# Another order for the instruction lists of the front phase of a four-part transformer kernel

## The chip, the cores and the metric

The kernel runs on one NeuronCore of a Trainium2 chip. A core has five engines with an instruction list each: TensorE (PE), VectorE (DVE), ScalarE (ACT), GpSimd (POOL) and the sync engine (SP), which here only starts transfers. An engine takes its own list strictly in order; engines meet at semaphores. The metric is device time in microseconds (us) of one launch. Three runs of the kernel before took 638.17, 638.5 and 638.55 us.

## The reference

Input is `x` of 16 sequences by 64 tokens by 256 features (1024 rows) and a context of the same size. Four blocks follow one another, each with a layer norm in front and a gate `tanh(g)` on what it adds to `x`:

```
x = x + tanh(g_xattn[0]) * attention_0(layernorm(x), mask, ctx)      # one head, 64 keys, new K and V fill the cache
x = x + tanh(g_ffn[0])   * ffn_0(layernorm(x))                       # ternary weights, tokens rounded to 8 bits
x = x + tanh(g_xattn[1]) * attention_1(layernorm(x), ctx)            # 16 query heads of 128, self and cross, fp8 rounding
x = x + tanh(g_ffn[1])   * experts(layernorm(x))                     # 7 routed experts, top 3, and a shared one
```

`ffn_0` is `h = silu(q(x) @ Wg) * (q(x) @ Wu)`, an RMS norm with a weight, and `q(h) @ Wd`. `q` rounds a row to integers by its largest magnitude; the weights are rounded to -1, 0 and 1 by their mean magnitude. In `attention_1` every head of q and k is layer-normed, and `ctx @ w_kv_x` gives the keys and values of the cross attention.

## The kernel before

The program has three phases with a barrier between them: `front` (lines 605 to 1414), two passes of `grouped_attention`, and the experts. The front computes the first attention and the ternary FFN, and beside them three things that the passes need: the rounded inputs `xq` of the first pass, the split weights of that pass (`weights.*`), and the context product (`context(e)`), whose 24 tiles go to memory over SP. The diff touches the front's five lists and nothing else.

The 1024 rows are handled as two groups `s` of four tiles `j`. Helper functions are one step each, and a list is a sequence of calls:

- PE: `turn` (transposes of the normed tokens, L1204), `project_qk` (L1214), `scores` (L1234), `project_v` (L1222), `turn_probs` (L1244), `attend` (L1251), `turn_integers` (L1265), `gate_up(s, n)` (n = 0 to 7, one half row-tile each, L1280), `turn_hidden` (L1294), `down` (L1306), `context(e)` (L1323), `turn_normed` (L1332).
- ACT: `keep_*` empties PSUM banks, `tern.column_sum` and `tern.scale` prepare the ternary weights, `weights.high` makes the upper part of a weight (L195), `gated` is the silu (L1057), `square` (L1064), `over_scale` (L1095).
- DVE: `ln.moments` and `ln.apply` are the layer norm, `weights.mean` (L178, L180) and `weights.low` (L202) prepare a weight, `context_mean` (L900, L902), `hidden(s, n)` multiplies silu and up (L863), `hidden_largest` (L868), `round_hidden` (L889), `add_attention` (L833), `add_ffn` (L895), `round_two` (L908 to L921).
- POOL: `ln.on_pool` (L555), `weights.centre` (L185), `weigh(s, j)` (h times the RMS weight, L750), `centre_context` (L755), `rms` (L759).
- SP: `dma_start` for all inputs, then the 24 stores of `kept`.

The waits that matter for the order: `hidden(n)` waits for `gated(n)`; `gated(n)` waits for `gate_up(n)` and for `hidden(n-2)`; `gate_up(n)` waits for `hidden(n-2)`, since two pairs of PSUM banks alternate. `context(e)` waits for `keep_context(e-2)`. `weigh(s, j)` waits for `square(s, j)`, and `hidden_largest(s, j)` for `weigh(s, j)`. `down(s, j)` needs `keep_hidden(s, j)`, which needs `turn_hidden` and that `round_hidden(s, j)`. `gate_up(0, 0)` needs `tern.clip` 0 and 1. `over_scale` needs `inv`, the reciprocal of the input scales.

Of the kernel before, what the change touches and what calls it, by code (L numbers as in the profile page):

```python
# [21 lines left out]
P = 128  # L22
# [582 lines left out]
def front(nc, t, k, weights, slots):  # L605
# [5 lines left out]
    with phase_semaphores(nc) as take, ExitStack() as c:  # L611
# [93 lines left out]
        def _(sp):  # L705
            source = t["x"].rearrange("(n p) e -> p n e", p=P)
            sp.dma_start(k['x'][:, 0:ST, :], source[:, 0:ST, :]).then_inc(x_loaded[0], 16)
            sp.dma_start(k['x'][:, ST:TILES, :], source[:, ST:TILES, :]).then_inc(x_loaded[1], 16)
# [8 lines left out]
            weights.load(sp, t, 0)  # L717
            sp.dma_start(mask[:], t['mask'].rearrange('(n p) s -> p n s', p=P)).then_inc(q['v_loaded'], 16)
            for n, src in enumerate(('L1_q_in_scale', 'L1_k_in_scale', 'L1_v_in_scale', 'L1_qx_in_scale')):
                sp.dma_start(ins[:, n * KT:(n + 1) * KT], t[src]).then_inc(q['ln_loaded'], 16)  # L720
            sp.dma_start(w_ctx[:, 2], t['L1_wkvxT'][:, 2 * CH:3 * CH].rearrange('(c p) f -> p c f', p=P)).then_inc(q[f'wctx_loaded{2}'], 16)
            sp.dma_start(wv[:], t['L0_WvT'].rearrange('(c p) f -> p c f', p=P)).then_inc(q['v_loaded'], 16)
            weights.load(sp, t, 1)
            sp.dma_start(w_ctx[:, 0], t['L1_wkvxT'][:, 0 * CH:1 * CH].rearrange('(c p) f -> p c f', p=P)).then_inc(q[f'wctx_loaded{0}'], 16)
            sp.dma_start(lnw[:], t['L0_lnw'].rearrange('(o n) -> o n', o=1).broadcast_to([P, INNER])).then_inc(q['lnw_loaded'], 16)
            sp.dma_start(bv[:], t['L0_bv'].rearrange('(o n) -> o n', o=1).broadcast_to([P, E])).then_inc(q['v_loaded'], 16)
            tern.on_sync(sp, t)
            weights.load_small(sp, t)
            weights.load(sp, t, 2)
            sp.dma_start(ctxT[:], t['ctxT'].rearrange('(c p) n -> p c n', p=P)).then_inc(q['ctx_loaded'], 16)  # L730
            weights.load(sp, t, 3)
            sp.dma_start(w_ctx[:, 3], t['L1_wkvxT'][:, 3 * CH:4 * CH].rearrange('(c p) f -> p c f', p=P)).then_inc(q[f'wctx_loaded{3}'], 16)
            sp.dma_start(w_ctx[:, 1], t['L1_wkvxT'][:, 1 * CH:2 * CH].rearrange('(c p) f -> p c f', p=P)).then_inc(q[f'wctx_loaded{1}'], 16)
            for n in range(4, len(weights.kinds)):
                weights.load(sp, t, n)
            for e, (tile, chunk) in enumerate(PRODUCTS):
                sp.wait_ge(q['ctx_kept'], e + 1)
                sp.dma_start(k['kvx'][tile, :, chunk * CH:(chunk + 1) * CH], kept[:, e % 4, :]).then_inc(stored[e % 4], 16)
# [6 lines left out]
        def _(pool):  # L745
# [24 lines left out]
            weights.centre(pool, 0)  # L770
            ln.on_pool(pool, 1)
            weights.centre(pool, 1)
            ln.on_pool(pool, 2)
            ln.on_pool(pool, 3)
            weights.centre(pool, 2)
# [3 lines left out]
            weights.centre(pool, 3)  # L779
            weights.centre(pool, 4)  # L780
            weigh(0, 2)
            weigh(0, 3)
            weigh(1, 0)
            centre_context(0)
            rms(0)
            weights.centre(pool, 5)
# [9 lines left out]
        def _(dve):  # L796
# [131 lines left out]
            weights.mean(dve, 0)  # L928
            ln.apply(dve, 1, lambda j: an[:, 1, j, :])
            weights.mean(dve, 1)  # L930
# [3 lines left out]
            divide(0)  # L934
            add_attention(0)
            ln.moments(dve, 2)
            dve.wait_ge(q['gate_made'], 1)
            weights.scale(dve)
# [4 lines left out]
            weights.low(dve, 0)  # L943
            product_scales(0)
            less_max(1)
            keep_values(1)
            round_tokens(0)
            tern.clip(dve, 0)
            divide(1)
            tern.clip(dve, 1)  # L950
            add_attention(1)
# [5 lines left out]
            weights.mean(dve, 2)  # L957
            hidden(0, 2)
            token_scales(1)
            hidden(0, 3)  # L960
            weights.low(dve, 1)
            round_tokens(1)
            weights.mean(dve, 3)
            hidden(0, 4)
            hidden(0, 5)
            weights.mean(dve, 4)
            hidden_largest(0, 0)
            hidden(0, 6)
# [12 lines left out]
            hidden_largest(0, 3)
            hidden(1, 2)
            mean_square(0)
            hidden(1, 3)
            hidden_largest(1, 0)
            hidden_scales(0)
            hidden(1, 4)
            hidden(1, 5)
            weights.low(dve, 2)
            round_hidden(0, 0)  # L990
            weights.low(dve, 3)
            hidden(1, 6)
            round_hidden(0, 1)
            hidden(1, 7)
            round_hidden(0, 2)
            round_hidden(0, 3)
            weights.low(dve, 4)
            mean_square(1)
            hidden_largest(1, 1)
            hidden_largest(1, 2)  # L1000
# [5 lines left out]
            round_hidden(1, 1)  # L1006
            ln.apply(dve, 4, lambda j: qn[:, 0, j, :])
            round_hidden(1, 2)
            round_hidden(1, 3)
            weights.low(dve, 5)  # L1010
            round_two(0)
# [7 lines left out]
        def _(act):  # L1019
# [81 lines left out]
            keep_qk(0, 1)  # L1101
            keep_tokens(1)
# [4 lines left out]
            tern.column_sum(act, 0)  # L1107
            tern.column_sum(act, 1)
            keep_qk(1, 0)
            tern.column_sum(act, 2)  # L1110
            keep_qk(1, 1)
            weights.high(act, 0)
# [11 lines left out]
            keep_context(3)  # L1124
            gated(0, 2)
            weights.high(act, 1)
            keep_context(4)
            gated(0, 3)
            keep_context(5)
            weights.high(act, 2)  # L1130
            gated(0, 4)
            gated(0, 5)
            square(0, 0)
            square(0, 1)
            keep_context(6)
            keep_context(7)
            gated(0, 6)
            square(0, 2)
            keep_context(8)
            gated(0, 7)  # L1140
            keep_integers(1)
            keep_context(9)
            weights.high(act, 3)
            gated(1, 0)
            square(0, 3)
            gated(1, 1)
            keep_context(10)
            square(1, 0)
            gated(1, 2)
            keep_context(11)  # L1150
            weights.high(act, 4)
            keep_context(12)
            gated(1, 3)
            keep_context(13)
            square(1, 1)
            gated(1, 4)
            gated(1, 5)
            weights.high(act, 5)
            keep_context(14)
            square(1, 2)  # L1160
            gated(1, 6)
            keep_context(15)
            keep_hidden(0, 0)
            gated(1, 7)
            square(1, 3)
            keep_hidden(0, 1)
            keep_hidden(0, 2)
            keep_context(EARLY)
            keep_context(17)
            keep_hidden(0, 3)  # L1170
            keep_context(18)
# [5 lines left out]
            over_scale(1)  # L1177
            keep_hidden(1, 2)
            weights.high(act, 6)
            keep_context(20)  # L1180
            keep_hidden(1, 3)
            over_scale(2)
            weights.high(act, 7)
            keep_context(21)
            over_scale(3)
            keep_context(22)
            keep_context(23)
# [1296 lines left out]
```

## Time and profile before

| what | value |
| --- | --- |
| median of three runs | 638.5 us |
| the profiled execution, its own time | 637.83 us |
| its span, first to last instruction | 636.1 us |
| busy PE, DVE, ACT, POOL | 582.5, 496.7, 370.2, 366.1 us |
| front, by the barrier's end | 0 to 145.1 us |
| DVE busy in 57.6 to 88.1 us | 29.72 of 30.5 us |
| mean granted clock of TensorE | 0.976 |

A row of the timeline gives start, length, engine and line, operation, what it writes and from what; in brackets stands how long the engine had been idle before it and what it waited for. Rows of equal instructions are merged (x2). "PEclk" is the share of full clock that was granted: 0.50 is 1.2 GHz and 1.00 is 2.4 GHz.

### The profile page before, as it was taken

What the parts mean: (1) busy time and instruction counts of PE and PEld (TensorE: products, weight loads), DVE (VectorE), ACT (ScalarE), POOL (GpSimd) and SP (SyncE); (2) the same over time, 40 slices, a digit from 0 to 9 for tenths busy, and PEclk for the clock granted to TensorE, in tenths of its full rate; (3) what the DMA queues carried; (4) which work ended last, traced back from release to release, by engine and by line L of the source; (5) the groups of instructions that cost most, each with busy time, mean ns of one, the idle gap of its engine ahead of it and who ended that gap; (6) DMA issues with size and microseconds to landing.
All of it is one profiled execution on the core that took longest, in us unless ns stands there. A gap on an engine that the chain in (4) does not pass through costs nothing.

```text
span 636.1 us, 10615 instructions
## 1 busy us (share of the span) xinstructions
PE 582.5 (92%) x3738; PEld 471.0 (74%) x3738; DVE 496.7 (78%) x924; ACT 370.2 (58%) x669; POOL 366.1 (58%) x299
## 2 busy tenths in 40 slices
PE   3999786978869999999998999999999999999996
PEld 1655333644558898888987898888889888888886
DVE  4488999886998999998979889999987956333333
ACT  1477675485666676776767765676666235434231
POOL 3100765303656878778778866766766733855431
PEclk9999898998969999999999999999999999999999
DMA  7981220114413112131085132322110100311001
GB/s 236 294 305 66 84 82 33 68 66 152 144 39 133 36 60 73 35 124 43 2 312 174 46 116 67 85 83 80 49 57 18 34 1 2 112 39 33 2 1 66
DMA packets 44564, 54.86 MB, mean 86 GB/s; under 512 B 8417, under 2 KB 30817, under 8 KB 44513
## 3 DMA queue, kind: packets, MB, share of 16 engines
q1 hardware_dynamic: 44512, 54.20, 26.1%
q8 instruction: 30, 0.49, 0.3%
q14 instruction: 22, 0.17, 0.1%
HBM read 41.60 MB, written 12.58 MB: 85 GB/s over the span
## 4 chain that ended last, share of the span: by engine, by line
PE 62%; DVE 5%; POOL 4%; ACT 3%; issue 2%; DMA 1%; DVEq 0%; POOLq 0%; ACTq 0%
PE g_proj L2220 12%; PE g_proj L2306 7%; PE g_scores L2261 6%; PE g_turn L2250 6%; PE g_op L2287 5%; PE g_op L474 2%; PE g_op L476 2%; PE g_op L475 2%; PE g_proj L459 2%; PE g_proj L461 2%; PE g_proj L460 2%; PE g_turn L2270 2%; POOL g_rs L1613 1%; PE g_turn L459 1%; PE g_scores L459 1%
## 5 line engine op out<-in xcount | busy, mean ns | idle before, releaser
L1613 POOL TENSOR_TENSOR g_rs<-g_ve,neg_half 128x4 f32<-128x4 f32 x80 | 83.5, 1048 | 37.8 <-DVE g_ve L1723 37.4
L1632 POOL TENSOR_TENSOR g_cat<-g_yb,g_kb 128x1024 fp32r<-128x1024 bf16 x32 | 71.0, 2226 | 41.1 <-DVE g_yb L1780 41.1
L2220 PE MATMUL g_proj<-w_hi,g_xqc 128*128 128x512 f32 x192 | 85.1, 443 | 1.5 <-DVE g_qn L1736 1.2
L2220 PE MATMUL g_proj<-w_lo,g_xqc 128*128 128x512 f32 x192 | 77.2, 402 | 0.0
L503 POOL TENSOR_TENSOR m_h_lo<-m_h,m_h_hi 128x512 fp32r<-128x512 f32 x32 | 41.4, 1296 | 57.1 <-ACT m_h_hi L490 57.1
L1723 DVE TENSOR_REDUCE g_ve<-g_sq 128x4 f32<-128x516 f32 x80 | 54.6, 684 | 18.4 <-ACT g_sq L1980 16.8
L2261 PEld LDWEIGHTS g_scores<-g_qkT 128*128 128x128 f32 x512 | 62.4, 196 | 8.1 <-issue 6.9
L2261 PE MATMUL g_scores<-g_qkT 128*128 128x64 f32 x512 | 62.8, 277 | 4.8 <-DVE g_ex L1746 4.8
L2250 PE MATMUL g_turn<-ident,g_qn 128*128 128x128 f32 x384 | 58.0, 278 | 1.3 <-DVE g_qn L1736 1.3
L1980 ACT ACTIVATE g_sq<-g_proj 128x512 f32<-128x512 f32 x80 | 47.7, 596 | 16.3 <-PE g_proj L2220 14.5
L2250 PEld LDWEIGHTS g_turn<-ident,g_qn 128*128 128x128 f32 x384 | 45.0, 143 | 10.8 <-DVE g_qn L1736 2.6
L1323 PE MATMUL f_bank<-f_w_ctx,f_ctxT 128*128 128x512 f32 x96 | 47.1, 622 | 1.8 <-ACT f_kept L1079 1.1
L490 ACT ACTIVATE m_h_hi<-m_h 128x512 fp32r<-128x512 f32 x32 | 20.2, 632 | 48.6 <-DVE m_h L497 48.6
L2220 PEld LDWEIGHTS g_proj<-w_hi,g_xqc 128*128 128x128 f32 x192 | 37.3, 194 | 10.2 <-DVE g_qn L1736 2.1
L2014 ACT ACTIVATE g_qkT<-g_turn,c_lnp 128x512 f32<-128x512 f32 x48 | 36.5, 777 | 14.2 <-PE g_turn L2250 14.2
L1736 DVE TENSOR_TENSOR g_qn<-g_proj,g_rs 128x512 f32<-128x512 f32 x64 | 43.7, 682 | 1.3 <-POOL g_rs L1613 1.3
L2287 PE MATMUL g_op<-g_pT,g_v 64*128 64x128 f32 x512 | 37.2, 285 | 5.5 <-ACT g_pT L2033 5.5
L513 DVE SCALAR_TENSOR_TENSOR x_res<-g_op,m_we,x_res 128x256 f32<-128x256 f32 x64 | 27.8, 478 | 17.8 <-PE g_op L476 17.8
L2287 PEld LDWEIGHTS g_op<-g_pT,g_v 64*128 64x128 f32 x512 | 31.1, 187 | 14.4 <-ACT g_pT L2033 10.0
L2220 PEld LDWEIGHTS g_proj<-w_lo,g_xqc 128*128 128x128 f32 x192 | 37.4, 195 | 5.5 <-issue 0.8
L555 POOL TENSOR_TENSOR ln_rstd<-ln_ve,neg_half 128x4 f32<-128x4 f32 x6 | 6.6, 1094 | 58.3 <-DVE ln_ve L542 58.3
L2014 ACT ACTIVATE g_qkT<-g_turn,x_lnp 128x512 f32<-128x512 f32 x48 | 36.2, 771 | 5.6 <-PE g_turn L2250 5.6
(247 smaller groups left out, 1662.4 us busy)
## 6 DMA issues: line engine op xcount, KB each, us to landing
kvx_rows<-f_kept SPq DMA_DIRECT2D x24, 256.0 KB, 2.4
g_ksq<-kvx_rows SPq DMA_DIRECT2D x8, 512.0 KB, 4.4
g_kraw<-kvx_rows SPq DMA_DIRECT2D x16, 256.0 KB, 3.2
g_v<-kvx_rows SPq DMA_DIRECT2D x8, 512.0 KB, 4.0
m_raw<-in_L_W SPq DMA_DIRECT2D x16, 256.0 KB, 3.0
c_raw<-in_L_wqT SPq DMA_DIRECT2D x4, 512.0 KB, 5.8
f_w_ctx<-in_L_wkvxT SPq DMA_DIRECT2D x4, 512.0 KB, 8.1
c_praw<-in_L_wprojT SPq DMA_DIRECT2D x4, 512.0 KB, 5.4
```

What stands on the lines that cost most here:

```text
L1323: last = T.matmul(context_bank(e)[:], ctxT[:, c_, tile * P:(tile + 1) * P], w_ctx[:, chunk, c_, :], start=c_ == 0, stop=c_ == KT - 1)
L1613: G.tensor_tensor(rs[:, at % NORMS, :], ve[:, at % NORMS, :], k["half"][:, 0:4], ALU.pow).then_inc(q["rs_done"], 1)
L1632: G.tensor_tensor(cat[:, h].rearrange("p h (b s) -> p b h s", b=2), yb[:, h, :].rearrange("p (b h s) -> p b h s", b=2, s=SEQ), kb[:, h, :] ...
L1723: V.tensor_reduce(ve[:, at % NORMS, :], sq[:, at % 2], AX.X, ALU.add).then_inc(q["ve_done"], 1)
L1736: V.tensor_tensor(qn[:, i % 2, :].rearrange("p (h d) -> p h d", d=D), bank(n, i)[:].rearrange("p (h d) -> p h d", d=D), bcast(rs[:, at % N ...
L1980: A.activation(sq[:, at % 2, :, 0:D], bank(n, i)[:].rearrange("p (h d) -> p h d", d=D), ACT.Square, scale=D ** -0.5).then_inc(q["sq_done"], 1)
L2014: A.activation(qkT[:, n % 2, at:at + 4, :], turns[TURN_BANK[i]][:].rearrange("p (h m) -> p h m", h=4), ACT.Identity, bias=lnp[:, w + 1:w + ...
L2220: last = T.matmul(bank(n, i)[:], xqc[:, n % 2, view * KT + c_, :], w[:, c_, :], start=c_ == 0 and part == 0, stop=c_ == KT - 1 and part == 1)
L2250: last = T.transpose(out, qn[:, i % 2, h * D:(h + 1) * D], k["ident"][:])
L2261: last = T.matmul(sp_[:, (g * 2 + b) * SEQ:(g * 2 + b + 1) * SEQ], qkT[:, n % 2, 2 * kv + b, :], qkT[:, n % 2, HEADS + kv, rows], start=Tr ...
L2287: last = T.matmul(op[:, b, g * P:(g + 1) * P], v[rows, n % 2, kv * D:(kv + 1) * D], pT[rows, h, g, :], start=True, stop=True)
L2306: last = T.matmul(proj[OUT_BANK][:, 0:E], cat[:, h, hd % (2 * GH), :], w[hd // 4][:, hd % 4, :], start=hd == 0 and part == 0, stop=hd == H ...
```

## The change

The calls of the front stay the same and are put into another order, on every engine. No instruction is added or removed. SP loads two weights and the mask before the second half of `x`, and the context and RMS weights last. The core of the diff:

```diff
@@ sync
             sp.dma_start(k['x'][:, 0:ST, :], source[:, 0:ST, :])
-            sp.dma_start(k['x'][:, ST:TILES, :], ...)
+            weights.load(sp, t, 0)
+            weights.load(sp, t, 1)
+            sp.dma_start(mask[:], ...)
             (lw, lb, g_xattn, g_ffn, wq, wk, bq, bk)
-            weights.load(sp, t, 0)
-            (mask, four ins, w_ctx 2, wv, weights 1, w_ctx 0, lnw, bv)
-            tern.on_sync; weights.load_small; weights 2; ctxT; weights 3; w_ctx 3, 1; weights 4 to 7
+            (wv, bv, weights 2, second half of x)
+            tern.on_sync; weights.load_small; four ins; weights 3; w_ctx 1, 2, 0; weights 4 to 7; ctxT; w_ctx 3; lnw
@@ gpsimd
             weights.centre(pool, 0)
+            weights.centre(pool, 1)
+            weights.centre(pool, 2)
             ln.on_pool(pool, 1)
...
@@ vector
             ln.apply(dve, 0, ...)
+            weights.mean(dve, 0)
+            weights.mean(dve, 1)
+            weights.mean(dve, 2)
             dve.wait_ge(x_loaded[1], 16)
             ln.moments(dve, 1)
...
             divide(0)
+            dve.wait_ge(q['gate_made'], 1)
+            weights.scale(dve)
             add_attention(0)
             ln.moments(dve, 2)
+            weights.mean(dve, 3)
             ln.apply(dve, 2, ...)
             largest(0)
+            context_mean(0)
             token_scales(0)
             tern.means(dve)
+            round_tokens(0)
             less_max(1)
             keep_values(1)
+            divide(1)
             weights.low(dve, 0)
+            add_attention(1)
...
             hidden(0, 7)
             hidden(1, 0)
+            weights.low(dve, 1)
             context_mean(1)
             hidden(1, 1)
...
             weights.low(dve, 5)
+            dve.wait_ge(q['ln_loaded'], 96)
+            V.reciprocal(inv[:], ins[:])
             round_two(0)
@@ scalar
             keep_qk(0, 1)
+            tern.column_sum(act, 0)
             keep_tokens(1)
...
-            tern.scale(act, 0)
             exponent(1)
             keep_probs(1)
+            tern.scale(act, 0)
+            weights.high(act, 1)
+            keep_context(0)
             tern.scale(act, 1)
-            keep_context(0)
             keep_context(1)
             keep_integers(0)
             keep_context(2)
+            keep_context(3)
+            weights.high(act, 2)
             gated(0, 0)
@@ tensor
             project_qk(0)
+            scores(0)
             turn(1)
-            scores(0)
...
             turn_probs(1)
-            context(0)
-            context(1)
             turn_integers(0)
             attend(1)
+            context(0)
+            context(1)
             context(2)
+            context(3)
             gate_up(0, 0)
-            context(3)
...
+            gate_up(1, 7)
             context(14)
             context(15)
-            gate_up(1, 6)
-            gate_up(1, 7)
             turn_hidden(0, 0)
+            context(EARLY)
+            context(17)
             turn_hidden(0, 1)
...
             turn_hidden(1, 2)
             down(1, 1)
+            context(21)
+            context(22)
             turn_hidden(1, 3)
             down(1, 2)
             down(1, 3)
-            context(22)
             context(23)
             turn_normed(1)
```

## Rows read from the trace of the kernel before

**Rows 1.** Windows over the front: length, busy (count) per engine, clock, DMA, GB/s

```profile
0.00:57.60 57.60, 44.75 (x169) 27.90 (x170) 35.21 (x103) 27.80 (x38) 9.79 (x17) 1.00 0.74 244
57.60:88.10 30.50, 26.82 (x82) 11.38 (x81) 29.72 (x40) 21.02 (x34) 15.95 (x7) 0.94 0.19 70
88.10:102.10 14.00, 10.44 (x34) 3.97 (x32) 13.86 (x20) 10.34 (x19) 9.43 (x6) 1.00 0.20 75
102.10:121.14 19.04, 14.65 (x79) 10.21 (x79) 17.65 (x25) 9.22 (x16) 8.72 (x4) 0.91 0.15 56
121.14:135.30 14.16, 13.41 (x85) 9.51 (x84) 11.12 (x33) 11.44 (x19) 1.44 (x1) 1.00 0.11 39
135.30:145.10 9.80, 4.36 (x15) 1.75 (x13) 8.37 (x33) 6.32 (x11) 1.01 (x1) 0.81 0.21 80
```

**Rows 2.** Timeline of SP: issue of three loads

```profile
5.30 0.43 SPq L716 DMA_DIRECT2D f_bk<-in_L_bk  x1
15.81 6.42 SPq L155 DMA_DIRECT2D c_insc<-in_L_q_in_scale  x1
28.44 0.47 SPq L730 DMA_DIRECT2D f_ctxT<-in_ctxT  x1
```

**Rows 3.** DMA issues: count, KB, us from issue to landing

```profile
f_bk<-in_L_bk SPq DMA_DIRECT2D x1, 1.0 KB, 4.8
f_mask<-in_mask SPq DMA_DIRECT2D x1, 256.0 KB, 6.2
```

**Rows 4.** Timeline of PE, first attention

```profile
12.69 6.58 PE L1214 MATMUL f_bank<-f_anT,f_wq 128*128 128x512 f32 x8 [2.61 <-ACT f_anT L1025]
22.55 1.04 PE L1204 MATMUL f_bank<-ident,f_an 128*128 128x128 f32 x8
51.05 1.89 PE L1251 MATMUL f_bank<-f_v,f_pT 128*128 128x256 f32 x8
```

**Rows 5.** Timeline of DVE, first attention and first product of the FFN

```profile
31.37 1.66 DVE L833 SCALAR_TENSOR_TENSOR x_res<-f_bank,f_rc,x_res 128x256 f32<-128x256 f32 x4 [0.40 <-PE f_bank L1251]
57.69 0.75 DVE L863 SCALAR_TENSOR_TENSOR f_h<-f_bank,f_du,f_silu 128x512 f32<-128x512 f32 x1 [1.77 <-ACT f_silu L1057]
```

**Rows 6.** Windows around the end of the loads, same columns as group 1

```profile
44.00:46.00 2.00, 1.92 (x10) 1.18 (x8) 1.72 (x4) 0.86 (x3) 0.00 (x0) 1.00 0.19 72
```

**Rows 7.** Timeline of ACT: scale of a ternary weight, table load, upper part of a weight

```profile
46.59 2.09 ACT L594 ACTIVATE f_raw<-f_raw,magic,tern_inverse 128x2048 f32<-128x2048 f32 x1
55.60 1.28 ACT L1057 ACT_TABLE_LOAD   x1 [0.31 <-PE f_bank L1280]
61.30 1.32 ACT L195 ACTIVATE w_hi<-c_raw,c_sc 128x512 fp32r<-128x512 f32 x2
```

**Rows 8.** DVE in 57.6 to 118.1 us, grouped by line: count, busy, mean ns

```profile
L178 DVE TENSOR_REDUCE c_sums<-c_raw 128x8 f32<-128x1024 f32 x4 | 4.8, 1206 | 0.0
```

**Rows 9.** Timeline of DVE beside running POOL instructions

```profile
69.77 1.84 DVE L180 TENSOR_SCALAR c_sums<-c_sums 128x8 f32<-128x8 f32 x1
78.87 2.73 DVE L602 TENSOR_SCALAR f_values<-f_values 128x2048 bf16<-128x2048 bf16 x1
89.35 3.46 DVE L868 TENSOR_REDUCE f_ah<-f_h 128x1 f32<-128x1024 f32 x3
102.72 3.50 DVE L202 SCALAR_TENSOR_TENSOR w_lo<-c_raw,c_sc,w_hi 128x512 fp32r<-128x512 f32 x2
```

**Rows 10.** Timeline of POOL in the same stretch

```profile
69.24 4.66 POOL L750 TENSOR_TENSOR f_h<-f_h,f_lnw 128x1024 f32<-128x1024 f32 x2 [3.88 <-ACT f_junk L1064]
73.85 3.91 POOL L185 TENSOR_TENSOR c_raw<-c_raw,c_sums 128x1024 f32<-128x1024 f32 x2
```

**Rows 11.** Timeline of PE, down products and contexts

```profile
109.36 2.56 PE L1323 MATMUL f_bank<-f_w_ctx,f_ctxT 128*128 128x512 f32 x4
112.63 1.91 PE L1306 MATMUL f_bank<-f_values,f_hT 128*128 128x256 bf16 x16
134.61 3.60 PE L1323 MATMUL f_bank<-f_w_ctx,f_ctxT 128*128 128x512 f32 x8
```

**Rows 12.** Window after PE's idle time, same columns as group 1

```profile
108.00:110.00 2.00, 2.00 (x9) 1.70 (x8) 2.00 (x4) 1.76 (x4) 0.53 (x1) 0.50 0.00 0
```

**Rows 13.** Timeline of DVE, last instructions of the front

```profile
143.02 0.75 DVE L921 TENSOR_TENSOR xq_all<-f_big,f_kb 128x512 bf16<-128x512 bf16 x2
```

More of the change, by code:

```diff
@@ L716, in _ @@
                 sp.dma_start(dst[:], t[src]).then_inc(q['qk_loaded'], 16)
-            weights.load(sp, t, 0)
-            sp.dma_start(mask[:], t['mask'].rearrange('(n p) s -> p n s', p=P)).then_inc(q['v_loaded'], 16)
+            sp.dma_start(wv[:], t['L0_WvT'].rearrange('(c p) f -> p c f', p=P)).then_inc(q['v_loaded'], 16)
+            sp.dma_start(bv[:], t['L0_bv'].rearrange('(o n) -> o n', o=1).broadcast_to([P, E])).then_inc(q['v_loaded'], 16)
+            weights.load(sp, t, 2)
+            sp.dma_start(k['x'][:, ST:TILES, :], source[:, ST:TILES, :]).then_inc(x_loaded[1], 16)
@@ L770, in _ @@
             weights.centre(pool, 0)
+            weights.centre(pool, 1)
+            weights.centre(pool, 2)
             ln.on_pool(pool, 1)
[L772 removed]
             ln.on_pool(pool, 2)
             ln.on_pool(pool, 3)
[L775 removed]
+            weights.centre(pool, 3)
             pool.wait_ge(q['lnw_loaded'], 16)
@@ L778, in _ @@
             weigh(0, 1)
-            weights.centre(pool, 3)
+            centre_context(0)
+            weigh(0, 2)
             weights.centre(pool, 4)
-            weigh(0, 2)
             weigh(0, 3)
             weigh(1, 0)
-            centre_context(0)
+            weights.centre(pool, 5)
             rms(0)
-            weights.centre(pool, 5)
             weigh(1, 1)
@@ L1006, in _ @@
             round_hidden(1, 1)
+            round_hidden(1, 2)
             ln.apply(dve, 4, lambda j: qn[:, 0, j, :])
-            round_hidden(1, 2)
             round_hidden(1, 3)
             weights.low(dve, 5)
+            dve.wait_ge(q['ln_loaded'], 96)
+            V.reciprocal(inv[:], ins[:]).then_inc(q['ins_done'], 1)
             round_two(0)
@@ L1106, in _ @@
             A.activation(k['gate'][:], gate_raw[:], ACT.Tanh).then_inc(q['gate_made'], 1)
-            tern.column_sum(act, 0)
             tern.column_sum(act, 1)
+            weights.high(act, 0)
             keep_qk(1, 0)
@@ L1177, in _ @@
             over_scale(1)
+            keep_context(20)
             keep_hidden(1, 2)
-            weights.high(act, 6)
-            keep_context(20)
             keep_hidden(1, 3)
+            keep_context(21)
             over_scale(2)
-            weights.high(act, 7)
-            keep_context(21)
             over_scale(3)
+            over_scale(4)
+            over_scale(5)
             keep_context(22)
             keep_context(23)
-            over_scale(4)
-            over_scale(5)
             over_scale(6)
@@ L1397, in _ @@
             turn_hidden(1, 0)
+            context(20)
             turn_hidden(1, 1)
@@ L1400, in _ @@
             turn_normed(0)
-            context(20)
             turn_hidden(1, 2)
+            down(1, 1)
             context(21)
-            down(1, 1)
+            context(22)
             turn_hidden(1, 3)
```

162 lines of the change are left out of this document (71 added, 91 removed).

## The prediction

> **What bounds the kernel now.** I read the page's totals first and then left them, because the lists change only ahead of the barrier at 145.1 us; what follows the barrier, 491 us, is the same program. So the views are: windows over the front, then each engine's timeline, then which wait ends last at each join. In the windows the reader is to see four stages [rows 1]. To 57.6 us PE is the engine with the least slack (44.75 busy) and DVE has 22 us free. From 57.6 to 102.1 us DVE is full (29.72 of 30.5, then 13.86 of 14.0) and PE waits for it. From 121.1 to 135.3 us PE is full (13.41 of 14.16). The last 9.8 us are a DVE chain again, which ends at 143.77 [rows 13]. An order can gain in two ways: move DVE work out of the full stretch into its free time, and keep PE busy while it waits for DVE so that less of its work stands in the tail.
>
> Part of DVE's fullness is no work. With a POOL instruction running, a DVE operation of 0.17 us takes 1.84 us, one of 0.7 us 2.73, and two `weights.low` pieces 3.50 instead of 1.40 [rows 9]; each ends when a POOL instruction does: 69.24 plus half of 4.66 is 71.57, and 69.77 plus 1.84 is 71.61 [rows 9, 10]. The three reductions at 89.35 run beside POOL at 1.15 each and pay nothing. So DVE's operations that read SBUF by two ports wait for the running POOL instruction, 2.33 us for a `weigh` and 1.95 for a `centre` [rows 10]. Summed over 57.6 to 118 us I read nine such waits, about 15 us. How the new order falls on POOL's instructions matters more than the order itself.
>
> **The change part by part.** I walk the new lists by hand with the durations of the rows, an engine starting a step at the later of its own end and the last wait.
>
> Loads. `wq`, `wk`, `bq`, `bk` move behind two weights and the mask: 0.75 MB more ahead and two more issues. Before, `bk` landed at 5.30 + 4.8 = 10.1 us [rows 2, 3], and `project_qk(0)` began at 12.69, released by ACT after 2.61 us of idleness [rows 4]. The 0.75 MB at some 330 GB/s (what the windows to 16 us move is near that) are 2.3 us, so 12.4: hidden by ACT's step, with 0.3 us left. Bounds: 0 to +1.0; I take 0. The mask took 6.2 us to land for 256 KB, and it now goes ahead of these loads [rows 3]. "DMA: Bandwidth & Descriptors" of the Trainium skill, section Specifications, has transfers under 512 B below line rate, and the mask's rows are 256 B long; if they cost double, the landing is 0.8 us later, so the start moves by 0.5 and the sum below would be 1.2 instead of 0.7. This trace doesn't isolate it.
>
> `ctxT` moves to the end. SP's stall at 15.81 (6.42 us) comes again some 3 us earlier, as 1 MB less stands in front; the small loads' issues then leave the queue empty as before. All 12.6 MB are in by about 44.3 us before, since the window 44 to 46 moves only 72 GB/s [rows 6]. `ctxT` then lands at about 45; `context(0)` comes at 49.5 in the new list. Free; bounds 0 to +1. The second half of `x` lands near 17.5 and `apply(1)` ends at 21.8, against 25.4 when `turn(1)` wants it. The three earlier `mean` and `centre` steps lie in DVE's idle time before 25.7. Free.
>
> `scores(0)` ahead of `turn(1)`. `scores(0)` started at 23.49, right when ACT had kept kT, and `turn(1)` had filled the gap for nothing (22.55, 0.94 to the next) [rows 4]. Now it stands behind and pushes `project_v(0)`, `attend(0)` and `project_qk(1)` by 0.94. `weights.scale` ahead of `add_attention(0)` adds to that: 31.37 [rows 5] becomes 32.8. ACT's first column sum falls in its wait for scores and costs nothing.
>
> `attend(1)` ahead of `context(0)` and `(1)`: 51.05 [rows 4] becomes 47.7, `add_attention(1)` ends at 51.0 instead of 53.9. This gain is not kept, since ACT is late next. `tern.scale(0)` now starts only after `keep_probs(1)`, at 47.45: scale 2.1, high(1) 1.2, keep 0.5, at 51.8 scale(1) 2.0, then three keeps and `keep_integers` to 57.0 (one short wait for `context(3)`), high(2) 1.2, table load 1.3, silu 0.7 [rows 7]. `hidden(0, 0)` starts at 60.2 against 57.69 [rows 5]: 2.5 late. In return DVE enters the full stretch with three means fewer, 3 x (1.21 + 0.17) = 4.1 us [rows 8].
>
> 58 to 89 us. DVE waits for silus 1.1 us more and meets POOL at mean(4) (1.7) and product_scales(1) (both pieces, 3.4 with a weigh and centre_context); clip(2) falls in POOL's idle time. `hidden(1, 0)` ends at 81.4 against 87.3, 5.9 earlier. But then come `low(1)` and `context_mean(1)`, which the old list had done by here, and `weigh(0, 2)`, `centre(4)` and `weigh(0, 3)` run back to back on POOL from 81.0. The pieces of low(1) wait for the first two of them (1.9 + 1.9), the mean's small piece 1.1. `hidden(1, 1)` ends at 89.7 against 88.1; mean(5), 1.4, is done already. So the 5.9 us shrink to 0.2 behind. This is the step that decides.
>
> 89 to 103 us. low(2) waits 1.5 + 1.0, low(3) 0.6; after `hidden(1, 5)` at 102.75 PE does `gate_up(1, 7)`, to 103.7 (102.1 before).
>
> PE's tail. `context(14)` and `(15)` now stand behind `gate_up(1, 7)`. A context is 1.72 at full clock (3.60 for two, with the overlap of 0.15), a down or a turn 0.9 [rows 11]. From 103.7 to the end of `down(0, 3)`: five contexts 8.6, four turns 3.6, four downs 3.6, 0.5 for the last keep: 16.3, so 120.0, and `add_ffn(0)` ends at 120.5 against 121.14. Before, two contexts fewer stood there, but PE sat idle 3.6 us for `round_hidden(0, 1)` and then ran at 1.2 GHz (clock 0.50, a context of 2.56) [rows 11, 12]; both go. Next, `context(22)` moves ahead of `turn_hidden(1, 3)`: four contexts 6.9, four turns and `turn_normed(0)` 4.5, four downs 3.6, 0.5 of waits: 15.5, so `add_ffn(1)` ends at 136.0 against 135.3 [rows 1]. The late reciprocal holds `over_scale(0)` back by about 0.4 us and delays keep(20); it lies beside PE's contexts. From there the DVE chain is as before, 8.5 us: 144.5 against 143.8.
>
> Sum: -0.6 at `add_ffn(0)`, +1.3 for the context moved ahead, so +0.7 at the barrier. The profiled execution took 637.83 us, 636.1 of them span; +0.7 is 638.5. The median of the runs is 638.5, 0.7 above it, so the forecast on that footing is 639.2. Bounds of the sum: -4.7 if low(1) and context_mean(1) meet no POOL instruction, +3 if the tail starts at half clock.
>
> **The rivals.** (1) Faster: the pieces slip past POOL. If `hidden(1, 0)` ends a microsecond earlier or `square(0, 2)` later, low(1) runs in 1.4 us, `hidden(1, 5)` ends near 98, and PE's tail, which is then bound by PE alone, moves with it one for one: up to -4.7, I take -3.5, 635.0. It decides at whether DVE reaches low(1) before POOL begins `weigh(0, 2)`. For it: the three means in idle time and 5.9 us of lead. Against it: POOL has as much work as before, and it follows the squares, so the two come together. Beside it stands "SBUF — State Buffer" of the Trainium skill, section SBUF: two separate sides: the shared pair is held for a whole instruction, whichever starts first. By that rule the piece pays whatever is left of POOL's instruction, as in the rows, and no less on average for being moved.
>
> (2) Slower: the clock. While DVE holds `hidden(1, 1)` back, PE has one gap of about 5 us (84 to 89.7) and small ones to 103. Before, gaps of 3.3 and 3.6 us were followed by about 4 us at 1.2 GHz [rows 1, 12], the second at the tail's start. If a low stretch falls behind 103.7 here, where PE has no slack, it costs half of 4 us: +2.0, together +2.7, 641.2. It decides at a gap of over 3 us just ahead of `turn_hidden(0, 0)`. Against: my walk has only gaps under 2 us there.
>
> (3) Slower: the ladder. gate_up, silu, hidden and the keeps wait for one another with contexts in between. If one more collision falls in 60 to 80 us or `bk` lands late, each 1 us is 1 us at the end, as nothing behind catches up: +2, 640.5.
>
> (4) The order changes nothing because the ends are bound by work that no order removes: within 0.3 of the sum; it cannot be told from the forecast. That lists don't do what they say I exclude: the sequence is the program's.
>
> **How the numbers follow.** Forecast 0.45, (1) 0.27, (2) 0.13, (3) 0.15. This kernel's measurement tells 0.2%, 1.3 us, from no change: 637.2 to 639.8. The forecast's own range is 637.0 to 641.0, and two thirds of it lie within the bound, the rest slower: same 0.30, slower 0.15. (1) gives 0.25 faster, 0.02 same; (2) 0.13 slower; (3) 0.11 slower, 0.04 same. I round to faster 0.26, same 0.35, slower 0.39. The range for 8 in 10 is 634.6 to 642.2: it takes in most of (1) and all of (2).
>
> **What would show it.** In the profile after: `project_qk(0)` at 12.7 (load step); `attend(1)` near 47.7 and `hidden(0, 0)` near 60.2 (ACT step); `hidden(1, 0)` ending near 81; low(1) of about 5 us instead of 1.4 (the deciding step; 1.4 to 2 means rival 1); `gate_up(1, 7)` near 103; PE clock 1.00 from 104 to 136; the barrier near 145.8. The forecast is wrong if DVE's collisions in 57 to 118 us sum to under 10 us or over 18, or if the stretch behind the barrier is not 491 us within 0.5.

## The result and the profile after

The changed kernel takes 634.82 us (median of 8 runs, 633.18 to 635.91), the kernel before, beside it on the same chip, 638.28 us (8 runs, 637.86 to 638.64). The ratio is 0.9945 with a 95% interval of 0.9936 to 0.9954: faster by 3.5 us or 0.55%. I had forecast 639.2, slower by 0.7: the result lies near the low end of my range (634.6 to 642.2), on the other side of no change.

The profiled execution of the changed kernel took 635.6 us (span 633.8, mean clock 0.978), against 637.83 (span 636.1) before. So the two profiles differ by 2.3 us of span: 3.03 us less up to the barrier's end (142.15 against 145.18) and 0.73 us more behind it (491.65 against 490.92).

The windows below are cut at the same events as those of before [rows 1], to within 0.3 us: start of `hidden(0, 0)`, end of `hidden(1, 1)`, end of `gate_up(1, 7)` (where PE's tail starts), ends of the two `add_ffn`, end of the front's work. The busy times are of PE, of PE's weight loads, of DVE, ACT and POOL, in this order.

```profile
0.00:59.97 59.97, 47.16 (x175) 29.28 (x177) 39.36 (x110) 30.66 (x43) 13.15 (x19) 1.00 0.73 239
59.97:86.63 26.66, 17.82 (x62) 7.13 (x61) 25.67 (x34) 17.38 (x28) 12.79 (x7) 1.00 0.13 50
86.63:100.68 14.05, 13.39 (x36) 5.71 (x38) 13.95 (x20) 9.53 (x17) 9.64 (x5) 0.88 0.20 75
100.68:117.19 16.51, 16.11 (x86) 10.44 (x85) 15.12 (x22) 12.46 (x23) 8.00 (x4) 1.00 0.26 97
117.19:132.26 15.07, 15.02 (x89) 10.24 (x88) 11.24 (x34) 10.70 (x19) 1.44 (x1) 1.00 0.11 43
132.26:142.10 9.84, 2.87 (x11) 1.28 (x9) 8.37 (x33) 4.94 (x9) 1.01 (x1) 0.79 0.19 70
```

Against [rows 1] the first stage is 2.4 us longer, but DVE does 4.2 us more work in it (39.36 busy against 35.21), about what the three moved means take (4.1). The full DVE stretch is 3.8 us shorter (26.66 against 30.50), the third stage equal, PE's first half of the tail 2.5 us shorter (16.51 against 19.04, clock 1.00 instead of 0.91), the second half 0.9 us longer, the last stage equal. The second stage holds less work, so its length alone proves nothing. DVE's busy time over the whole front says more: the same instructions take 113.71 us instead of 115.94. What changed are the lengths of pieces that meet POOL; from `hidden(0, 0)` to 118 us their waits sum to about 13 us, against about 15.5 before. So some 2.2 us of waiting are gone. From `hidden(0, 0)` on DVE is then busy for 6.4 us less than before (74.35 against 80.73): 4.2 moved ahead and 2.2 no longer waited.

The timeline of DVE in the changed kernel, at `hidden(0, 0)` and at the instructions which pay for a POOL instruction:

```profile
59.97 0.75 DVE L863 SCALAR_TENSOR_TENSOR f_h<-f_bank,f_du,f_silu 128x512 f32<-128x512 f32 x1 [2.57 <-ACT f_silu L1057]
80.77 3.51 DVE L202 SCALAR_TENSOR_TENSOR w_lo<-c_raw,c_sc,w_hi 128x512 fp32r<-128x512 f32 x2
85.44 0.62 DVE L902 TENSOR_SCALAR f_ctx_sums<-f_ctx_sums 128x8 f32<-128x8 f32 x1
86.63 1.73 DVE L872 TENSOR_SCALAR f_ms<-f_ssq 128x4 f32<-128x4 f32 x1
91.86 1.86 DVE L202 SCALAR_TENSOR_TENSOR w_lo<-c_raw,c_sc,w_hi 128x512 fp32r<-128x512 f32 x2
95.43 2.49 DVE L202 SCALAR_TENSOR_TENSOR w_lo<-c_raw,c_sc,w_hi 128x512 fp32r<-128x512 f32 x2
```

and POOL beside `weights.low(1)`:

```profile
80.83 2.90 POOL L750 TENSOR_TENSOR f_h<-f_h,f_lnw 128x1024 f32<-128x1024 f32 x1 [6.94 <-ACT f_junk L1064]
83.69 2.34 POOL L185 TENSOR_TENSOR c_raw<-c_raw,c_sums 128x1024 f32<-128x1024 f32 x1
```

The reader is to see who comes first. DVE starts the first piece of `low(1)` at 80.77, POOL its `weigh(0, 2)` 0.06 us later. The piece runs at once, the `weigh` waits for it (2.90 us instead of 2.33 [rows 10]), and the second piece waits for the `weigh` and ends 0.55 us behind it, at 84.28. One wait, not two.

The timeline of PE, at the start of its tail and ahead of the front's last step:

```profile
99.50 1.04 PE L1280 MATMUL f_bank<-f_values,f_xqT 128*128 128x512 bf16 x4 [0.47 <-DVE f_h L863]
100.38 3.60 PE L1323 MATMUL f_bank<-f_w_ctx,f_ctxT 128*128 128x512 f32 x8
137.36 1.67 PE L1332 MATMUL f_bank<-ident,f_xn 128*128 128x128 f32 x8 [3.90 <-DVE f_xn L547]
```

`gate_up(1, 7)` is done at 100.4 (102.1 before), and from there PE works nearly without a gap to the last context.

Behind the barrier 0.7 us goes again. PE is idle for 3.90 us ahead of `turn_normed(1)`, as `context(22)` no longer stands there (2.18 before), and the clock is low from 138 us on instead of 142. The first 10 us of the pass, from the barrier on, before and after:

```profile
145.18:155.18 10.00, 9.87 (x25) 5.15 (x26) 7.28 (x12) 6.45 (x13) 3.62 (x5) 0.85 0.61 180
```

```profile
142.15:152.15 10.00, 10.00 (x20) 5.03 (x20) 6.07 (x10) 5.42 (x12) 2.73 (x5) 0.70 0.57 161
```

The granted clock is 0.70 of full instead of 0.85, and 20 matmuls are counted instead of 25. That the moved `context(22)` brings this is not shown, and three runs below speak against it. `held_low` and `low_early` have the same 3.90 us of idleness, but 0.85 and 0.83 in their first 10 us, and 491.16 and 491.23 us behind the barrier. `late_ctx22` has the context back and 2.18 us of idleness, but 0.75 and 491.39. Two profiles of the changed kernel itself differ by 0.45 us there.

### The profile page after: what moved, and what is told of

The parts are those of the page before. It is cut to its first block, busy times and chain, and to the rows that moved or that the text cites. A ratio compares the mean times of both kernels' runs of the same rounds, so it can differ in the third digit from the quotient of the medians.

```text
span 633.8 us, 10612 instructions
## 1 busy us (share of the span) xinstructions
PE 580.7 (92%) x3735; PEld 471.2 (74%) x3738; DVE 492.8 (78%) x924; ACT 369.4 (58%) x669; POOL 365.9 (58%) x299
## 4 chain that ended last, share of the span: by engine, by line
PE 65%; DVE 5%; POOL 3%; ACT 2%; issue 2%; DMA 1%; DVEq 0%; POOLq 0%; ACTq 0%
PE g_proj L2220 13%; PE g_proj L2306 8%; PE g_scores L2261 7%; PE g_turn L2250 6%; PE g_op L2287 5%; PE g_op L474 2%; PE g_op L475 2%; PE g_op L476 2%; PE g_proj L459 2%; PE g_proj L461 2%; PE g_proj L460 2%; PE g_turn L2270 2%; PE g_op L2228 1%; PE g_turn L459 1%; PE g_scores L459 1%
## 5 line engine op out<-in xcount | busy, mean ns | idle before, releaser
L1980 ACT ACTIVATE g_sq<-g_proj 128x512 f32<-128x512 f32 x80 | 47.7, 596 | 18.0 <-PE g_proj L2220 16.4
L1323 PE MATMUL f_bank<-f_w_ctx,f_ctxT 128*128 128x512 f32 x96 | 44.9, 604 | 0.9 <-ACT f_kept L1079 0.9
```

The source lines that it names most:

```text
L1323: last = T.matmul(context_bank(e)[:], ctxT[:, c_, tile * P:(tile + 1) * P], w_ctx[:, chunk, c_, :], start=c_ == 0, stop=c_ == KT - 1)
L1980: A.activation(sq[:, at % 2, :, 0:D], bank(n, i)[:].rearrange("p (h d) -> p h d", d=D), ACT.Square, scale=D ** -0.5).then_inc(q["sq_done"], 1)
```

## The experiments

All kernels but `means_early` and `before_tail` are the changed kernel with one edit; these two are the kernel before with one part of the change. Theory A in the expectations is that the front's length follows how DVE's operations fall on POOL's instructions; the rivals are the moved work itself, PE's order in the tail, and the clock. One number needs a word. The first eight matmuls of `project_qk(0)` start between 12.54 and 12.85 us and take 5.19 to 6.68 us, from execution to execution, and everything behind them up to the barrier shifts with it. So I compare two intervals that don't contain this length: **lead**, the start of `hidden(0, 0)` less the length of those eight matmuls, and **rest**, from `hidden(0, 0)` to the barrier's end. All times below are us.

| kernel | first 8 matmuls | lead | rest | DVE busy in the front | median (runs) | ratio, 95% interval |
| --- | --- | --- | --- | --- | --- | --- |
| before | 6.58 | 51.11 | 87.49 | 115.94 | 638.28 (8) | 1 |
| after | 6.60 | 53.37 | 82.18 | 113.71 | 634.82 (8) | 0.9945, 0.9936 to 0.9954 |
| again | 6.66 | 53.36 | 82.18 | 113.71 | 634.36 (5) | 0.994, 0.9928 to 0.9952 |
| held_low | 6.24 | 53.34 | 84.76 | 116.30 | 636.99 (12) | 0.9978, 0.997 to 0.9987 |
| late_ctx22 | 5.19 | 53.39 | 81.73 | 113.72 | 634.46 (5) | 0.9936, 0.9923 to 0.9949 |
| means_early | 5.43 | 54.50 | 84.90 | 113.64 | 637.57 (11) | 0.9985, 0.9976 to 0.9993 |
| pool_early | 6.68 | 53.38 | 82.41 | 113.94 | 635.6 (6) | 0.9957, 0.9944 to 0.997 |
| low_early | 6.39 | 53.39 | 81.19 | 112.71 | 634.02 (5) | 0.9938, 0.9926 to 0.9949 |
| turn_first | 5.40 | 53.78 | 82.30 | 113.71 | 634.9 (5) | 0.9947, 0.9935 to 0.9959 |
| tail_ctx_first | 5.65 | 53.45 | 85.54 | 113.30 | 637.36 (11) | 0.9997, 0.9986 to 1.0008 |
| held_pool | 5.31 | 53.44 | 82.45 | 113.91 | 635.97 (12) | 0.996, 0.9945 to 0.9974 |
| before_tail | 5.70 | 51.10 | 92.15 | 116.12 | 641.78 (6) | 1.0043, 1.0026 to 1.0059 |
| both | 6.67 | 53.65 | 80.76 | 112.79 | 634.77 (5) | 0.9942, 0.993 to 0.9954 |
| both_high2 | 6.25 | 52.58 | 81.58 | 112.51 | 633.0 (4) | 0.9916, 0.9903 to 0.9929 |

By these intervals the change costs 2.26 us of lead and brings 5.31 of rest. One kernel's lead holds something else as well: in `both` the eight matmuls started at 12.85 us, released by the load of `bk`.

**again.** The changed kernel with no edit, as the measure of what an equal list repeats.

> The changed kernel once more, unedited, as the base of the three others. In its first profile weights.low(1) began at 80.77 us, 0.06 us ahead of POOL's weigh(0, 2) at 80.83, and took 3.51 us. Theory A (the gain hangs on which of the two comes first there): low(1) takes 3.5 us again where DVE is first and about 5.1 us where POOL is first, and the front's end (142.15 us in the first profile) moves by the difference. Theory B (the gain is the DVE work moved into idle time, not the meeting): front's end within 0.5 us of 142.15 whichever is first. Median near 634.8 us.

Lead, rest and DVE's busy time repeat to 0.01 us. Ahead of the barrier only the first matmuls vary; behind it the two profiles differ by 0.45 us (491.65 and 492.10).

**held_low.** One reduction of 0.41 us on DVE just ahead of `low(1)`, nothing else:

```diff
             hidden(1, 0)
+            dve.wait_ge(q['lnw_loaded'], 16)
+            V.tensor_reduce(scratch[:], lnw[:, 0:256], AX.X, ALU.max)
             weights.low(dve, 1)
```

> The changed kernel with one reduction more on DVE, of 128x256 elements into a scratch tile, just ahead of weights.low(1): about 0.4 us by the 1.21 us of one of 128x1024. Theory A: low(1) now comes after POOL has begun weigh(0, 2), its two pieces wait for weigh(0, 2) and centre(4), it ends near 86.5 us instead of 84.28, and the front ends 2 us or more later: median 637. Theory B: 0.4 us on DVE's full stretch, at most 0.4 us at the end: median 635.2.

DVE, and POOL beside it, in that kernel:

```profile
80.39 0.41 DVE L976 TENSOR_REDUCE f_scratch<-f_lnw 128x1 f32<-128x256 f32 x1
80.71 4.93 DVE L202 SCALAR_TENSOR_TENSOR w_lo<-c_raw,c_sc,w_hi 128x512 fp32r<-128x512 f32 x2
```

```profile
80.44 2.36 POOL L751 TENSOR_TENSOR f_h<-f_h,f_lnw 128x1024 f32<-128x1024 f32 x1 [6.94 <-ACT f_junk L1067]
```

Now POOL is first by 0.27 us, and both pieces wait: `low(1)` takes 4.93 us instead of 3.51. `context_mean(1)` pays 1.07 instead of 0.62, `low(2)` 3.04 instead of 1.86, `low(3)` 3.32 instead of 2.49; only the small piece at L872 gets its 1.6 us back (0.15). The rest grows by 2.58 us, DVE's busy time by 2.59, of which 0.41 is the added work, and the median lies 2.2 above that of the changed kernel, as theory A had it. This is the situation my walk had assumed, and it costs more than half of the whole gain.

**pool_early.** POOL's `centre(4)` ahead of `weigh(0, 2)`, so that it runs while DVE is at hiddens:

```diff
+            weights.centre(pool, 4)
             weigh(0, 2)
-            weights.centre(pool, 4)
             weigh(0, 3)
```

> The changed kernel with POOL's centre(4) ahead of weigh(0, 2) instead of behind it, nothing else. POOL idles from 73.9 to 80.8 us there, so the centre runs in that gap and costs nothing; behind weigh(0, 2) POOL is then free sooner, and DVE's small mean-square piece (1.73 us in the changed kernel) and context mean piece (0.62) find it idle more often. Theory A (DVE's waits for POOL in the full stretch set the time): front's end 1 to 2 us earlier, median 633.3, DVE busy in the front 1 to 2 us less than 113.7. Theory B (POOL's order has no part in it): median as the changed kernel, 634.6.

The small piece at L872 falls from 1.73 to 0.15, but `low(2)` rises to 3.04 and `low(3)` to 2.72. Nothing is gained: rest 82.41. The expected 1 to 2 us did not come; `low(1)` itself kept its 3.51 us, so this run says nothing on that meeting.

**held_pool.** POOL held back ahead of `weigh(0, 2)` by four fills of an unused tile, so that `low(1)` is surely first:

```diff
     def weigh(s, j):
         (wait for square(s, j))
+        if (s, j) == (0, 2):
+            for i in range(4):
+                G.memset(scratch[:, i, :], 0.0)
```

> The mirror of holding DVE: the changed kernel with four small POOL writes (memset of 128x256 each, about 1 us in all by the 0.95 us of one of 128x1024) ahead of weigh(0, 2), after its wait. POOL gets more work and is later. Theory A (the meeting of low(1) and weigh(0, 2) sets the time): both pieces of low(1) pass before weigh(0, 2) starts, low(1) takes 1.4 us instead of 3.5, hidden(1, 1) starts 0.5 to 1 us earlier than 26.0 us after hidden(0, 0), and the time is up to 1 us shorter in spite of the work added. Rival: a later POOL only delays hidden_largest(0, 2) and the rest, and the time is 0 to 1 us longer.

DVE's `low(1)` and `low(2)`, and POOL's fills and `weigh(0, 2)`:

```profile
79.55 1.41 DVE L202 SCALAR_TENSOR_TENSOR w_lo<-c_raw,c_sc,w_hi 128x512 fp32r<-128x512 f32 x2
88.54 3.96 DVE L202 SCALAR_TENSOR_TENSOR w_lo<-c_raw,c_sc,w_hi 128x512 fp32r<-128x512 f32 x2
```

```profile
79.59 1.06 POOL L753 MEMSET f_scratch<- 128x256 bf16 x4 [6.92 <-ACT f_junk L1068]
80.62 2.56 POOL L754 TENSOR_TENSOR f_h<-f_h,f_lnw 128x1024 f32<-128x1024 f32 x1
```

`low(1)` is at its free length, also beside the fills, and `hidden(1, 1)` comes 24.4 us after `hidden(0, 0)` instead of 26.0. But `low(2)` pays 3.96, `low(3)` 2.69 and L872 1.28, and the rest ends at 82.45, no better than with no edit. Theory A in the narrow form, "`low(1)` decides", is refuted by this kernel. In the wide form, that the sum of all meetings counts, it holds within the new list: against the changed kernel the rest moves by 2.58 for 2.59 of DVE's busy time (`held_low`), 0.23 for 0.23 (`pool_early`), 0.27 for 0.20 (here) and -0.99 for -1.00 (`low_early`, next).

**low_early.** `low(1)` far ahead, between `hidden(0, 6)` and the reductions of `h`:

```diff
             hidden(0, 6)
+            weights.low(dve, 1)
             hidden_largest(0, 0)
...
             hidden(1, 0)
-            weights.low(dve, 1)
             context_mean(1)
```

> The changed kernel with weights.low(1) on DVE ahead of hidden_largest(0, 0) instead of behind hidden(1, 0): it runs at 76.5 us, where POOL is idle, in 1.4 us instead of 3.5. Theory A: 2.1 us less of waiting; the context mean's small piece then meets weigh(0, 2) or centre(4) and gives 1 to 1.5 of it back; front's end 0.5 to 1.5 us earlier, median 633.7. Rival: hidden(0, 7) and hidden(1, 0) come 1.4 us later and PE and ACT follow them, so the time is as the changed kernel or up to 1 us longer.

`low(1)` takes 1.40 us at 76.29, 2.1 less than in the changed kernel; `context_mean(1)` takes 1.73 instead of 0.62 for its small piece at 83.16, so 1.1 goes back: DVE's busy time falls by 1.00, the rest by 0.99.

**means_early.** The kernel before with three of the moved means alone:

```diff
             weights.scale(dve)
+            weights.mean(dve, 2)
...
             largest(0)
+            weights.mean(dve, 3)
+            context_mean(0)
...
-            (the same three at their old places)
```

> The kernel before with one thing of the change: on DVE alone, weights.mean(2), weights.mean(3) and context_mean(0) (4.1 us) stand behind moments(2) and largest(0), in DVE's slack before 57 us. Theory B (moved work): DVE's full stretch ends up to 4.1 us sooner, PE's tail follows, and two thirds or more of the change's gain come from this alone: 635 to 636 us. Theory A: how the pieces then meet POOL decides; anything from 634 to 639, and the sum of DVE's waits for POOL in 57 to 118 us, about 15 us before, changes by as much as the time does not follow the 4.1.

DVE's busy time falls by 2.30, as much as by the whole change, and the rest by 2.59, but the lead grows by 3.39: in the old list these steps stand in front of work that ACT and PE wait for. By the intervals the sum is a loss of 0.80, by the medians a gain of 0.15% (up to 0.24% by the interval, 1.5 us). Either way the moved means alone, in the old list, do not bring the change's gain: theory B had 635 to 636. It also shows that DVE's busy time alone doesn't set the time: it falls as in the changed kernel, and the front is no shorter.

**tail_ctx_first.** PE's `context(14)` and `(15)` back ahead of `gate_up(1, 6)`. The edit does more than its expectation says: `context(13)`, which the changed list has between `gate_up(1, 6)` and `(1, 7)`, goes ahead of both too, and on ACT the keeps of 13 and 14 and `weights.high` 4 and 5 go ahead of `gated(1, 6)`:

```diff
             context(12)
-            gate_up(1, 6)
             context(13)
-            gate_up(1, 7)
             context(14)
             context(15)
+            gate_up(1, 6)
+            gate_up(1, 7)
             turn_hidden(0, 0)
```

> The changed kernel with context(14) and context(15), and their keeps, ahead of gate_up(1, 6) and (1, 7) again, as in the kernel before. My walk had them cost 3.4 us in PE's tail. Theory 1 (they bind): add_ffn(0) ends up to 3 us earlier, median 632 to 633. Theory 2 (they fill PE's time while DVE is behind; ahead of gate_up(1, 6) they make hidden(1, 6) late): hidden(1, 6) starts 1 to 2 us later than at 100.0, add_ffn(0) ends no more than 0.5 us sooner, median 634.3 to 636.

PE's contexts 11 to 15, and DVE at `hidden(1, 6)`:

```profile
92.01 8.75 PE L1323 MATMUL f_bank<-f_w_ctx,f_ctxT 128*128 128x512 f32 x20
102.38 0.75 DVE L863 SCALAR_TENSOR_TENSOR f_h<-f_bank,f_du,f_silu 128x512 f32<-128x512 f32 x1 [3.59 <-ACT f_silu L1057]
```

DVE waits 3.59 us for a silu whose product PE did only after five contexts in a row; ACT was itself idle for 1.98 us ahead of that silu, so its own moved steps don't hold it. The rest grows by 3.36, and the whole gain of the change is gone (ratio 0.9997); at 637.36 that is worse than either theory had it. So the place of these three contexts is necessary for the gain. What 14 and 15 alone are worth no run shows; with one context of 1.72 us fewer the wait would be some 1.9 us, by estimate.

**before_tail.** The same two contexts moved in the list of before, alone:

```diff
-            context(14)
-            context(15)
             gate_up(1, 6)
             gate_up(1, 7)
+            context(14)
+            context(15)
             turn_hidden(0, 0)
```

> The kernel before with context(14) and context(15), and their keeps, behind gate_up(1, 7), as the change has them; nothing else. In the changed kernel the opposite edit cost 2.9 us, since hidden(1, 6) then waited for its gate_up. In the kernel before hidden(1, 6) stands behind low(2), round_hidden(0, 0) and low(3) on DVE and does not wait for PE. Theory 1 (the placement is a gain by itself): 1 us or more faster, under 637.4 us. Theory 2 (it pays only where DVE reaches hidden(1, 6) before PE has done it): PE's tail has 3.4 us more behind gate_up(1, 7), partly in its 3.6 us gap, and the time is the same to 2 us longer: 638.3 to 640.3.

PE at the last `gate_up`, and DVE at `add_ffn(0)`:

```profile
99.31 3.27 PE L1280 MATMUL f_bank<-f_values,f_xqT 128*128 128x512 bf16 x8 [4.77 <-DVE f_h L863]
```

```profile
123.55 0.48 DVE L895 SCALAR_TENSOR_TENSOR x_res<-f_bank,f_od,x_res 128x256 f32<-128x256 f32 x1 [4.70 <-PE f_bank L1306]
```

In the old list DVE is late here, so PE idles for 4.77 us where the contexts had stood, and still for 3.29 us at 107 us (3.64 before). The granted clock is 0.74 from 100 to 104 us and 0.53 from 112 to 116, and the tail is two contexts longer. Slower by 0.43%, rest +4.66, more than either theory had. So the place behind `gate_up(1, 7)`, which the gain needs in the new list, costs 4.66 us in the old one.

**late_ctx22.** `context(22)` back behind `down(1, 3)`:

```diff
             context(21)
-            context(22)
             turn_hidden(1, 3)
             down(1, 2)
             down(1, 3)
+            context(22)
             context(23)
```

> The changed kernel with context(22) behind down(1, 3), as in the kernel before. My walk has PE's tail bind add_ffn(1), so one context of 1.72 us fewer ahead of it brings the front's end 1.3 to 1.7 us forward: median 633.3. Rival: the DVE chain with the late reciprocal and round_two binds, and at most 0.3 us is won: median 634.6.

The rest falls by 0.45, not by the 1.3 that I had booked for the step: with the context gone from there, PE waits 0.50 us for `keep_hidden(1, 2)` and 0.66 for DVE (`add_ffn(1, 0)`, behind `round_two(0)`). The medians differ by less than the intervals.

**turn_first.** `turn(1)` back ahead of `scores(0)`:

```diff
             project_qk(0)
+            turn(1)
             scores(0)
-            turn(1)
```

> The changed kernel with turn(1) ahead of scores(0) on PE again. The step cost 0.77 us at attend(0) (30.89 us against 30.12 before). If that is carried to the end, as my walk had it, the front ends 0.8 us earlier: median 633.9. Rival: POOL, ACT and DVE all move by the same 0.8, the meetings stay, but the weight loads or the first column sum don't, and the slack in front of hidden(0, 0) eats it: median 634.6.

PE at `turn(1)`:

```profile
22.41 1.32 PE L1204 MATMUL f_bank<-ident,f_an 128*128 128x128 f32 x8 [1.01 <-DVE f_an L547]
```

`apply(1)` comes late in the new list, as the second half of `x` is loaded later, so `turn(1)` would wait 1.01 us for it. The swap of the change avoids just that: lead 53.78 without it, 53.37 with it, where the expectations had it lose 0.8 us or nothing. The medians don't resolve it.

**both and both_high2.** `low_early` and `late_ctx22` together, and then also ACT's `weights.high(2)` from ahead of the first silu to behind the second:

```diff
             keep_context(3)
-            weights.high(act, 2)
             gated(0, 0)
             gated(0, 1)
+            weights.high(act, 2)
```

> The changed kernel with weights.low(1) ahead of hidden_largest(0, 0) and context(22) behind down(1, 3). Each alone shortened the stretch from hidden(0, 0) to the front's end, by 1.0 and 0.45 us. If they add up: 80.7 us for it instead of 82.2, median 633.0 to 633.5. If both remove the same wait: 81.2, median 634.

> As the one before, with ACT's weights.high(2) behind gated(0, 1) instead of ahead of gated(0, 0), where DVE waits 2.57 us for the first silu. hidden(0, 0) then starts 1.2 us earlier. If the rest follows: median 632. If the meetings of DVE and POOL fall worse: anything to 635.

`both` has a rest of 80.76, the two edits' 0.99 and 0.45 added, but its first matmuls took 6.67 us in the profile, and its median, 634.77, shows nothing of it (633.0 to 633.5 expected). With `high(2)` behind, the first silu is no longer late: DVE's wait at `hidden(0, 0)` falls from 2.57 to 1.65 us and the lead to 52.58. The rest gives 0.82 of it back. At 633.0 us (ratio 0.9916, interval 0.9903 to 0.9929) this version beats both kernels: it is 5.4 us under the kernel before, measured beside it (638.44), and its interval lies under that of the change. That rests on four runs.

## Why the prediction was wrong

**Loads, right.** `project_qk(0)` at 12.57 against my 12.7. The mask took 7.7 us to land instead of 6.2 and `bk` 3.0 instead of 4.8 [rows 3]; nothing waited for them in this profile. The margin was thin: in `both` the start waited for `bk`, until 12.85. "DMA: Bandwidth & Descriptors" of the Trainium skill, section Specifications, has transfers under 512 B below line rate. The start 0.5 us later that I had worked out for the mask's narrow rows did not come.

**`scores` ahead of `turn`: shift right, account wrong.** `attend(0)` came 0.77 us later (0.94 foretold), but I took the old place of `turn(1)` for free. With `apply(1)` at 22.9 it isn't.

**ACT's step, right.** `attend(1)` 47.18 (47.7; 51.05 before [rows 4]), `hidden(0, 0)` 59.97 with a wait of 2.57 us for the silu (60.2).

**58 to 81 us, right.** `hidden(1, 0)` ended at 80.85 (81.4). The two collisions that I had named, at mean(4) and product_scales(1), are there: the pieces took 1.55 and 3.19 us (1.7 and 3.4 foretold).

**"The pieces of low(1) wait for the first two of them (1.9 + 1.9), the mean's small piece 1.1": the step that failed.** My walk had POOL's `weigh(0, 2)` at 81.0 and DVE at 81.4. POOL came at 80.83, 0.2 us earlier, and DVE at 80.77, 0.6 earlier, ahead by 0.06 us. `low(1)` paid 2.1 us, not 3.8, and the mean 0.45, not 1.1. From there to `hidden(1, 5)` I had 8.0 us of waits in all, and 5.7 came. Not all of it was as I had placed it: `low(2)` paid 0.5 instead of 2.5, `low(3)` 1.1 instead of 0.6, and the small piece at L872 paid 1.6, where I had none. The sum is 2.3 us less; with the 0.6 us earlier arrival that is 2.9 of the 3.4 us by which `hidden(1, 5)` was early (99.4 against 102.75); the other 0.5 is spread over steps that I had rounded. The walk's two arrival times were off by no more than 0.6 us, but the quantity they were used for jumps by 2 us on less than that, as held_low shows. I had called the step deciding and then priced it on one side. It is not the whole miss: `held_low`, where POOL is first as I had assumed, takes 636.99 us, still 2.2 under my 639.2. "SBUF — State Buffer" of the Trainium skill, section SBUF: two separate sides, says that whichever starts first has the shared pair for its whole instruction. The trace agrees where POOL had been idle (80.77 against 80.83). Where POOL came straight from another instruction the recorded starts don't tell who holds the pair: DVE's piece at 71.97 has the earlier start by 0.03 us and still waited for all of POOL's instruction.

```profile
71.97 1.94 DVE L856 TENSOR_SCALAR f_du<-f_am,tern_mean 128x4 f32<-128x4 f32 x1
```

```profile
72.00 1.89 POOL L755 TENSOR_TENSOR f_w_ctx<-f_w_ctx,f_ctx_sums 128x1024 f32<-128x1024 f32 x1
```

I had cited the rule and concluded from it that the move saves nothing on average, which doesn't follow for two fixed lists.

**PE's tail: the rate right, one step of reasoning wrong.** From `gate_up(1, 7)` to the end of `add_ffn(0)` I had 16.8 us, and 16.8 was measured, at clock 1.00 as foretold; so the 3.3 us between my 103.7 and the measured 100.4 went through to 117.19 one for one. `add_ffn(1)` followed 15.1 us later (15.5). What I had missed is the other end of moving `context(14)` and `(15)`: I counted their 3.4 us as a cost in the tail, beside the idle time and clock that go. Ahead of `gate_up(1, 6)`, together with `context(13)`, they made DVE wait 3.59 us. "+1.3 for the context moved ahead" was too dear by 0.9.

**Behind the barrier, wrong by 0.7.** I had 491 within 0.5 and had called a miss of that a sign of being wrong; it is 491.65, and 490.95 to 492.1 in the kernels that were tried.

**Rivals and chances.** Rival (1) named the mechanism, the point of decision and 635.0; it came out in part, DVE first for one piece of two: `low(1)` took 3.51 us, neither my 5 nor the rival's 1.4 to 2. That its 635.0 lies so near 634.82 is partly luck: it takes 3.5 us off the 638.5 of before, while its bound of 4.7 counts from my walk (102.75 to 98). It had 0.27 and the forecast 0.45; faster had 0.26 in all. Rival (2), the clock, came in the changed kernel only from 86 to 90 us (0.68 and 0.50, behind 2.90 us of idle PE), where PE waits for DVE, and not ahead of the tail; before_tail shows it there in the old list. My sign for the collisions, under 10 us or over 18, was too wide: they sum to about 13, and the forecast was wrong all the same.

**What stays open.** The profiles differ by 2.3 us and the medians by 3.5. The start's spread could make that up, since 1.4 us of it reach the barrier, but not every run has a profile, and why the kernel before spreads over only 0.8 us in its eight runs I can't say. What brings the 0.7 us behind the barrier is open. So is how the gain divides between moved work, shorter waits and PE's tail: the means tried alone and the contexts undone don't add up to it.

## What to carry to other kernels

Where two engines hold each other up, as DVE and POOL do here, a hand-written order is worth what its meetings sum to, and a nudge of 0.4 us can move that sum by 2: give such a step a chance for each side and not a price on one, and don't expect that curing one meeting cures the sum. Parts of a reordering have to be tried in the new list, by undoing them: putting three contexts back ahead of the last products cost 3.4 us there, and moving two of them away cost 4.7 us in the old one. Low-priority work for a slack engine belongs behind the last product that the full engine waits for, if nothing else of that engine's list is late by then.

## What the runs showed of the hardware

The same eight matmuls take from 5.19 to 6.68 us in different executions, at nearly the same start (PE, late_ctx22 and the changed kernel):

```profile
12.59 5.19 PE L1214 MATMUL f_bank<-f_anT,f_wq 128*128 128x512 f32 x8 [2.61 <-ACT f_anT L1025]
```

```profile
12.57 6.60 PE L1214 MATMUL f_bank<-f_anT,f_wq 128*128 128x512 f32 x8 [2.61 <-ACT f_anT L1025]
```

In both the first two take 2.04 to 2.05 us, 1.02 each; the next eight, of the same shape, take 3.60 us together, 0.45 each; in the shorter group more of the eight run at the faster rate. The granted clock in the records is 1.00 all along, so it does not show this step. And an engine that waits for the other doesn't lose only its own place: a waiting POOL instruction gets in between two pieces of DVE (80.83 above), and a piece of 0.16 us can take 1.73. Fills by POOL, which only write, did not hold DVE's two pieces up (79.59 above, 1.41 us for both).
